# Project and output stages pipelined over the sequences, and the wide layer's q and k in two fp32r parts instead of three bf16 parts

## What is computed

```python
def wide(x, Wq, Wk, Wv, Wff, bff):            # 16 heads of 8 features, B, T, D = 4, 1024, 128 here
    q = x @ Wq.T * (1.0 / sqrt(D));  k = x @ Wk.T;  v = x @ Wv.T       # x is the layer norm of the residual
    scores = einsum('bqhd,bkhd->bhqk', q, k)                            # per head 1024 x 1024
    return einsum('bhqk,bkhd->bqhd', softmax(scores), v).reshape(B, T, D) @ Wff.T + bff

def nested(x, ...):                           # 8 heads of 16 features; x is the layer norm of the residual
    for e in range(4):                        # token block e of 256 uses only the first 128 >> e features
        xn = layernorm(x_e, norm_w, norm_b);  m = 128 >> e
        q_e = xn[..., :m] @ q_w[:, :m].T + q_b     # k and v alike
    attn = softmax(q k^T * D ** -0.5) v       # over all 1024 tokens, per head
    return x + attn_e[..., :m] @ o_w[:m, :m].T + o_b[:m]        # x here is the layer norm too
```

## Time and profile before

| what | value |
|---|---|
| median of 3 runs | 3489.55 us (3488.01 to 3509.23) |
| the profiled execution, its time | 3490.88 us |
| its span | 3489.2 us |
| mean granted TensorE clock | 0.886 of full |
| TensorE busy | 3009.2 us (86%) |
| VectorE busy | 2549.8 us (73%) |
| ScalarE busy | 2145.4 us (61%) |
| GpSimd busy | 274.4 us (8%) |

### The profile page before, as it was taken

The page is one execution under the profiler, slowest core; times in us unless marked ns, Lnnn a source line. Parts: engine busy times, 40 slices in busy tenths (PEclk is TensorE's granted clock), DMA queues, the critical chain, the costliest instruction groups (busy, mean ns, idle before and its releaser), DMA issues. The chain is left out here.

```text
span 3489.2 us, 54392 instructions
## 1 busy us (share of the span) xinstructions
PE 3009.2 (86%) x19914; PEld 1749.3 (50%) x19914; DVE 2549.8 (73%) x3990; ACT 2145.4 (61%) x3771; POOL 274.4 (8%) x373
## 2 busy tenths in 40 slices
PE   6757999848999999856999979979999777769998
PEld 4533444422333333332444457668888555558886
DVE  5657999389999999556999434447777777767776
ACT  2214888515988888712888711228888444458887
POOL 0060000050000000050000001020000000020000
PEclk9956999767999999955999968969999888879999
DMA  1042221021000010033221010021111000021111
GB/s 27 5 100 52 38 38 20 5 83 27 20 20 20 20 21 19 2 65 91 38 38 20 2 26 1 0 61 47 46 46 46 5 1 0 1 74 46 46 46 58
DMA packets 76544, 115.13 MB, mean 33 GB/s; under 512 B 13552, under 2 KB 38160, under 8 KB 76304
## 3 DMA queue, kind: packets, MB, share of 16 engines
q1 hardware_dynamic: 76304, 111.97, 13.6%
HBM read 85.72 MB, written 25.43 MB: 32 GB/s over the span
## 5 line engine op out<-in xcount | busy, mean ns | idle before, releaser
L729 DVE TENSOR_REDUCE nested_a_halves<-banks 128x2 f32<-128x1024 f32 x512 | 617.3, 1222 | 62.5 <-PE banks L825 59.4
L779 ACT ACTIVATE nested_a_p<-banks 128x512 f32<-128x512 f32 x1024 | 553.7, 597 | 116.1 <-PE banks L855 97.1
L729 DVE TENSOR_REDUCE wide_a_halves<-banks 128x2 f32<-128x1024 f32 x512 | 593.4, 1216 | 33.3 <-PE banks L825 33.3
L779 ACT ACTIVATE wide_a_p<-banks 128x512 f32<-128x512 f32 x1024 | 554.0, 598 | 45.2 <-PE banks L855 33.9
L1524 DVE TENSOR_TENSOR mix_e_h_low<-mix_e_h,mix_e_h_high 128x512 fp32r<-128x512 f32 x512 | 349.6, 688 | 174.9 <-ACT mix_e_h_high L1630 166.9
L1647 ACT ACTIVATE mix_e_h<-banks,mix_b_folded 128x512 f32<-128x512 f32 x512 | 353.7, 691 | 103.4 <-PE banks L1701 103.0
L868 PE MATMUL banks<-nested_a_p,nested_values 128*32 128x256 f32 x4096 | 326.5, 398 | 0.0
L868 PE MATMUL banks<-wide_a_p,wide_values 128*32 128x256 f32 x4096 | 321.4, 392 | 0.0
L1630 ACT ACTIVATE mix_e_h_high<-mix_e_h 128x512 fp32r<-128x512 f32 x512 | 319.3, 624 | 0.0
L825 PE MATMUL banks<-nested_k_stack,nested_q_stack 48*128 48x512 f32 x1024 | 270.6, 523 | 39.0 <-DVE nested_a_halves L729 20.9
L855 PE MATMUL banks<-nested_q_stack,nested_k_stack 50*128 50x512 f32 x1024 | 252.0, 422 | 10.9 <-ACT nested_a_p L779 9.9
(11 more groups left out here) (366 smaller groups left out, 4469.3 us busy)
## 6 DMA issues: line engine op xcount, KB each, us to landing
mix_e_gate<-mix_gates_t SPq DMA_DIRECT2D x128, 256.0 KB, 3.1
nested_q_stack<-nested_q_parts SPq DMA_DIRECT2D x96, 128.0 KB
nested_q_parts<-nested_p_q_cut SPq DMA_DIRECT2D x16, 512.0 KB
nested_k_parts<-nested_p_k_cut SPq DMA_DIRECT2D x16, 512.0 KB
nested_k_stack<-nested_k_parts SPq DMA_DIRECT2D x32, 256.0 KB
wide_q_stack<-wide_q_parts SPq DMA_DIRECT2D x192, 32.0 KB
nested_k_stack<-nested_k_parts SPq DMA_DIRECT2D x32, 128.0 KB
mix_raw_w<-L_ffn_w_t SPq DMA_DIRECT2D x8, 512.0 KB, 7.6
```

Of the source, the lines that this page charges most:

```text
L729: dve.tensor_reduce(halves[:, half, i, 2 * a:2 * a + 2], bank[:, at:at + 2, :], AX, ALU.max).then_inc(maxed, 1)
L779: act.activation(p[:, kt % 4, j, :], bank[:, ST + n % RING, :], ACT.Exp, scale=scale).then_inc(probs, 1)
```

## The change

In all three layers the project and output stages are written out over the sequences and keep two buffers of each tile. VectorE normalises two sequences ahead; GpSimd's fills are gone, and ScalarE writes the ones (`ones`, three instructions of 2048 columns, and `fill_pads`) instead; ScalarE cuts the high part of q and k directly out of PSUM (`cut_high`) and VectorE makes the rest from PSUM (`cut_rest`), so the whole copies are gone; in the nested layers `first` and GpSimd's addition of it become eight ScalarE instructions a sequence (`grow_rows`). TensorE turns sequences 0 and 1 before it projects 0. SyncE stores 0 and 1, then loads 0 and 1, then stores 2 and 3. The output stage turns straight out of `mixed`, with two sets of PSUM banks.

The wide layer is given fp32r: its q and k are two parts and three products, 3 x 8 = 24 rows (26 with the shift), still in tiles of 64 rows; a load is 10 DMAs instead of 18, and a sequence's stores four DMAs of 512 KB. Its score and shifted matmuls have as many columns, and as many of them are issued, as before.

```diff
@@ class Heads @@
-        self.span = min(n for n in (32, 64, 128) if n >= self.rows + 2)
+        self.span = min(n for n in (64, 128) if n >= self.rows + 2)
...
-        self.mixed = core.sbuf(ctx, "mixed", [P, self.total, TILES, self.gw])
+        self.mixed = core.sbuf(ctx, "mixed", [P, B, TILES, D])
...
-        self.parts_out = core.sem("parts_out")
+        self.parts_out = [core.sem(f"parts_out{k}") for k in range(2)]
@@ project_stage, SyncE @@
                 store(0)
-
-                sp.wait_ge(ones_set, 1)
-                sp.wait_ge(parts_out, 32 * hd.parts)
+                store(1)
+                sp.wait_ge(ones_set, hd.SLOTS)
+                sp.wait_ge(parts_out[0], 32 * hd.parts)
                 for n in range(2):
                     hd.load(sp, n)
-                with sp.Fori(1, B) as it:
-                    store(it)
+                for b in range(2, B):
+                    store(b)
@@ project_stage, GpSimd @@
-                values = hd.values[:].rearrange("p n i c -> p (n i) c")
-                pool.memset(values, 0.0).then_inc(v_set, 1)
...
-                pool.memset(ones, 1.0).then_inc(v_set, 1)
...
-                pool.memset(hd.plain(hd.k_stack[:]).rearrange("r k s t -> r (k s t)"), 1.0).then_inc(ones_set, 1)
...
+                for b in range(B):
+                    factors(b)
                 pool.wait_ge(w_in, 16 * NW)
...
+                for b in range(B):
+                    add_bias(b)
@@ project_stage, VectorE @@
-                def cut_parts(it, n, whole):
...
-                    dve.wait_ge(qk_copied, it * 4 + 2 * (n + 1))
-                    wait_past(dve, parts_out, it * 32 * hd.parts)
-                    dve.tensor_copy(parts[n][:, 0, :], whole[:]).then_inc(cut, 1)
-                    dve.wait_ge(cut, done + 1)
-                    if hd.parts == 2:
-                        dve.tensor_tensor(parts[n][:, 1, :], whole[:], hd.plain(parts[n][:, 0, :]),
-                                          ALU.subtract).then_inc(cut, 1)
-                        return
...
+                def cut_rest(b, n):
+
+                    for c in range(chunks):
+                        done = 4 * b + 2 * n + c
+                        dve.wait_ge(high_cut, done + 1)
+                        high = hd.plain(parts[n][:, b % 2, 0, cols(c)])
+                        whole = bank[:, 2 + 2 * n + c, :]
+                        if hd.parts == 2:
+                            wait_past(dve, parts_out[b % 2], b // 2 * 32 * hd.parts)
+                            dst = parts[n][:, b % 2, 1, cols(c)]
...
+                            dve.tensor_tensor(dst, whole, high, ALU.subtract).then_inc(rest_cut, 1)
...
+                moments_of(0)
+                moments_of(1)
+                normalise(0)
+                moments_of(2)
+                moments_of(3)
+                normalise(1)
+                dve.wait_ge(w_in, 16 * NW)
+                for b in range(B):
+                    cut_rest(b, 0)
+                    cut_rest(b, 1)
...
+                    if b + 2 < B:
+                        normalise(b + 2)
+                    store_values(b)
@@ project_stage, ScalarE @@
+                def grow_rows(b):
+
+                    act.wait_ge(factored, (b + 1) * FACTORS)
+                    act.wait_ge(normed, (b + 1) * TILES)
+                    for i in range(TILES):
+                        row = x[:, b * TILES + i, :]
+                        act.activation(row, row, ACT.Identity, bias=fall[:, b, i:i + 1],
+                                       scale=grow[:, b, i:i + 1]).then_inc(grown, 1)
+
+                def cut_high(b, n):
+
+                    wait_past(act, parts_out[b % 2], b // 2 * 32 * hd.parts)
+                    for c in range(chunks):
+                        act.wait_ge(projected, b * 6 + (2 * n + c + 1))
+                        dst, src = parts[n][:, b % 2, 0, cols(c)], bank[:, 2 + 2 * n + c, :]
...
+                            act.activation(dst, src, ACT.Copy).then_inc(high_cut, 1)
...
+                for k in range(hd.SLOTS):
+                    ones(hd.k_stack[:, k], [hd.slabs, T]).then_inc(ones_set, 1)
+                act.wait_ge(w_in, 16 * NW)
+                copy_turned(0)
+                copy_turned(1)
+                for b in range(B):
+                    if masked:
+                        grow_rows(b)
+                    for n in range(2):
+                        cut_high(b, n)
...
+                    if b + 2 < B:
+                        copy_turned(b + 2)
...
+                    fill_pads(b)
@@ project_stage, TensorE @@
+                pe.wait_ge(w_in, 16 * NW)
+                turn(0)
+                turn(1)
+                for b in range(B):
+                    project(b)
+                    if b + 2 < B:
+                        turn(b + 2)
@@ attend_stage, SyncE (and the same on ScalarE) @@
-                sp.wait_ge(hd.parts_out, 32 * hd.parts * B)
+                for k in range(2):
+                    sp.wait_ge(hd.parts_out[k], 16 * hd.parts * B)
@@ output_stage @@
-                        dve.tensor_copy(m_[:, :, g * hd.gw:(g + 1) * hd.gw], src).then_inc(staged, 1)
...
+                            src = bank[:, 4 + b % 2 * 2 + c, (lo - 4 * c) * P:(hi - 4 * c) * P].rearrange(
...
+                            last = pe.transpose(bank[:, b % 2 * 2 + c, i * P:(i + 1) * P], hd.mixed[:, b, 4 * c + i, :],
+                                                core.ident[:])
...
+                turn(0)
+                turn(1)
@@ plan @@
-            lambda: heads_layer(core, "wide", 16, wide, False, BF16),
+            lambda: heads_layer(core, "wide", 16, wide, False, F32R),
```

More of the change, by code:

```diff
@@ L519, in _ @@
-                pool.wait_ge(v_set, 2)
-                pool.memset(hd.plain(hd.k_stack[:]).rearrange("r k s t -> r (k s t)"), 1.0).then_inc(ones_set, 1)
-                pool.wait_ge(ones_set, 1)
-                with pool.Fori(1, B - 1) as it:
-                    residuals(it)
-                    factors(it + 1)
-                residuals(B - 1)
-                pool.wait_ge(residual, B * TILES * (2 if masked else 1))
+                        row = x[:, b * TILES + i, 0:m]
+                        pool.tensor_tensor(row, row, out_bias[:, 0:m], ALU.add).then_inc(biased, 1)
@@ new lines, in cut_rest @@
+                def cut_rest(b, n):
[7 more added lines that the diff above has]
+                            dst = parts[n][:, b % 2, 1, cols(c)]
+                        else:
+                            wait_past(dve, last_cut, 2 * b + n - 1)
+                            wait_past(dve, second_cut, 2 * b + n - 1)
+                            dst = rest[:, n, cols(c)]
+                        if masked:
+                            bias = (q_bias, k_bias)[n]
+                            dve.scalar_tensor_tensor(dst, whole, bias[:], high, ALU.add,
+                                                     ALU.subtract).then_inc(rest_cut, 1)
+                        else:
+                            dve.tensor_tensor(dst, whole, high, ALU.subtract).then_inc(rest_cut, 1)
@@ L565, in store_values, with cut_last @@
+                def cut_last(b, n):
+                    dve.wait_ge(second_cut, 2 * b + n + 1)
+                    wait_past(dve, parts_out[b % 2], b // 2 * 32 * hd.parts)
+                    dve.tensor_tensor(parts[n][:, b % 2, 2, :], rest[:, n, :], parts[n][:, b % 2, 1, :],
+                                      ALU.subtract).then_inc(last_cut, 1)
+                def store_values(b):
                     for c in range(2):
-                        dve.wait_ge(projected, it * 6 + (5 + c))
+                        dve.wait_ge(projected, b * 6 + (5 + c))
@@ new lines, in cut_second, with fill_pads @@
+                def cut_second(b, n):
+                    act.wait_ge(rest_cut, 4 * b + 2 * n + 2)
+                    act.activation(parts[n][:, b % 2, 1, :], rest[:, n, :], ACT.Copy).then_inc(second_cut, 1)
+                def fill_pads(b):
+                    pads = hd.values[:, b * hd.groups:(b + 1) * hd.groups].rearrange(
+                        "p g i (j r) -> p (g i j) r", r=32)[:, :, hd.width:32]
+                    ones(pads, [hd.groups * TILES * hd.GROUP, 32 - hd.width]).then_inc(pads_set, 1)
@@ L795, in _ @@
                 copy_shifts(0)
-                act.wait_ge(hd.parts_out, 32 * hd.parts * B)
+                for k in range(2):
+                    act.wait_ge(hd.parts_out[k], 16 * hd.parts * B)
                 for u in range(UNITS):
@@ L954, in _ @@
             def _(act):
-                with act.Fori(0, B) as it:
+                for b in range(B):
                     for c in range(2):
-                        act.wait_ge(turned, it * 2 + (c + 1))
-                        act.wait_ge(projected, it * 2)
-                        act.activation(m_t[:, c * BANK:(c + 1) * BANK], bank[:, c, :], ACT.Copy).then_inc(copied, 1)
+                        act.wait_ge(turned, b * 2 + (c + 1))
```

(23 more changed lines are left out.)

241 lines of the change are left out of this document (110 added, 131 removed).

## The result

The changed kernel takes 3865 us (median of 4 runs, 3852.63 to 3865.74) where the kernel before takes 3495.6 (4 runs). The ratio is 1.104, with a 95% interval of 1.100 to 1.109: slower by a tenth. Its profiled execution took 3852.63 us, the fastest of the four, with a span of 3850.9 us, 361.7 more than before.

A forecast was written before the change was run, and what follows sets the result against it. TensorE was taken to bound the attention loops nearly throughout, waits the project stages. To the profiled 3490.9 us came +486 for the wide loop at the low clock and -98 for the pipelining: 3879 us, range 3600 to 3950.

The forecast's parts named there:

- The clock: Wide attention loop: starts at 0.50 and, with 24 and 26 rows, doesn't rise; low clock throughout given 0.75.
- the mixture keeps whichever level it finds: Nested1's and the wide layer's last units: 50-row pairs and value matmuls stay at the clock they find, 0.50 or 1.00.
- the fall in nested1's last unit: Nested1's attention loop: the clock, full before, fell to 0.50 after one pause of TensorE.
- The price at the low clock: Wide attention loop: 2.16 us a step, 36.1 us a unit, 1142 us against 656, so +486 us.
- fp32r at full clock: Wide attention loop: fp32r costs 1.53 us a unit over 32 units, +49 us, if nothing else moves.
- rival 1: Wide loop: the clock rises as now, fp32r costs +49 us, the rest saves 98, total 3442 us; chance 0.13.
- The project stages of the nested layers: Nested1 and nested2: first exponential 28 us earlier in each, bounds 10 and 36, waiting for all stores to land.
- The wide project stage: Wide layer: first exponential at 787 us instead of 814.6, 27 us gained, bounds 12 and 34.
- The output stages: All three layers: no staging copy and overlapping sequences gain 5 us each, bounds 2 and 9, from TensorE's idle time.
- The chances: Whole kernel: faster by over 1% 0.17, within 1% 0.02, slower 0.81.
- the full-clock cases: Wide loop at full clock: with the cost of fp32r (3442 us, chance 0.13) or without it (3393 us, 0.04).

The follow-up runs named there:

- pads_48: The changed kernel with 24 rows of zeros (ones in one k row) after the wide layer's 24, giving 48 and 50 rows: 3412.2 us, ratio 0.975.
- pads_first4: The changed kernel with wide rows moved up 32 partitions over zeros, units 0 to 3 contracting 56 and 58 rows, the rest 24 and 26: 3799.7 us, ratio 1.088.
- wide_bf16: The changed kernel with the wide layer back in three bf16 parts (48 and 50 rows), everything else as changed: 3374.6 us, ratio 0.965.
- pads_36: The changed kernel with 12 rows of zeros added in the wide layer, giving 36 and 38 rows: 3714.0 us, ratio 1.063.
- twice_48: The changed kernel with the wide layer's three products loaded twice (48 rows of data) and the exponentials' scale halved: 3447.7 us, ratio 0.985.

## Why the prediction was right

The forecast of 3879 us lies 14 us above the median and 26 above the profiled execution on which the sum was made.

- **The clock.** The step that carried the forecast, that the loop with 24 and 26 rows doesn't rise from the level at which it starts, held: 0.50 over 1148.7 us. What follows the rows was shown by pads_48, where rows of zeros alone bring the clock back. The reason that I gave beside it, that the mixture keeps whichever level it finds, was wrong: pads_first4 handed a high clock to a step with 24 and 58 rows, and it was lost after 18 us without a pause. So the loop most likely stays low because it can't hold the other level, and not only because it starts there. What makes the clock fall stays open. I had put the fall in nested1's last unit on one pause of TensorE; in wide_bf16 and pads_48 nested1's last unit, the same instructions, has the same pause (busy 3.23 of 4.00 us from 612 to 616) and stays at 1.00. And in the kernel before the clock came back there from 656 us on (0.96), with the mixture unchanged. That I drew the right conclusion for the new loop from this stretch was partly luck.
- **The price at the low clock.** 2.16 us a step, 36.1 us a unit: measured 2.16 and 36.16. The loop was put at 1142 us and took 1148.7, +492 instead of +486.
- **fp32r at full clock**, the term of rival 1, was 1.53 us a unit and +49; pads_48 measured 1.54, and +51 for the loop, which also stood longer at the low clock. Rival 1's 3442 us was the time with the clock up; pads_48, which is that case, took 3412 (its profiled execution 3423). The stages gained about 40 us beyond my figure, and that execution gave back 20 of them in nested2's loop (373.1 us against 352.9), where the clock rose 35 us after the first exponential.
- **The project stages of the nested layers**: -28 each, measured -30.5 and -30.2. The size was right and the path was not. I had the first exponential wait for the last store to land, then for load(2)'s issues and the shift rows behind them. The last store had landed by 258.2, earlier than the 263 to 270 given, and load(2)'s issues were over at 262.7, yet SyncE then waited until 266.7 for the shift rows. The chain was the issue of the last store (over at 242.8), 0.8 us to the first score pair, and 29.8 us of row maxima, shift rows and first shifted pairs, as long as before. What got shorter by 30.5 us is the stretch up to the first score pair, 82.8 us instead of 113.3. That the path through the landing, worked out in advance, gave nearly the same time is luck.
- **The wide project stage**: -27, measured -39.8, beyond my bound of -34. This is the term that was most mis-sized. I had the drain end near 775 and the first exponential at 787 us on the old time axis; it came 81.3 us after the stage's start, which is 774.8 on that axis. The rate was taken from nested1 (145 to 158 GB/s); here stores and loads moved at 219 GB/s between 664.0 and 709.6 us, and all had landed 63 us into the stage, at 756.7 on the old axis. And as in the nested layers it was the issue of the last store, over at 697.2, that let the first score pair start at 697.9. Against wide_bf16 some 12 us of the gain come with two parts instead of three, which I had counted only as bytes and not as work for ScalarE and VectorE.
- **The output stages**: -5 each, measured -15.6, -8.9 and -13.8. I bounded the gain by TensorE's idle time of 7.8 and 9.1 us and forgot that in the nested layers its busy time at a clock of 0.60 would shrink as well: after the change the stretches stand at 0.95, 0.88 and 0.91, and TensorE's busy time in nested1's fell from 21.4 to 12.3 us. The wide one stood at 0.93 before, and its gain is mostly idle time (9.1 to 1.6 us).
- **Not foreseen**: nested2's loop took 7.7 us longer, with its clock rising about 31 us after the first exponential instead of 9. Its instructions are the same in all variants, and it took from 352.9 us (the kernel before) to 373 (pads_48, pads_36); differences of up to 20 us between two executions here can be this alone.
- **The chances**: the cases that I put down as slower add up to 0.83 and not 0.81, and the 0.02 for no change would have to come out of the 0.17 of the full-clock cases.

The sum was close because its largest term was right. The stages gained 139 us and not 98, which put into the sum gives 3838; the wide loop (+6.4), nested2's loop (+7.7) and the rest (+0.4 together) bring it to the 3852.6 of the profiled execution. The other three executions took some 12 us more than that one.

**The rule of the Trainium skill** ("TensorE: Matmul & The Clock Gate", Part 1: The HAM clock gate), by which the gate follows how busy TensorE has been, does not describe this loop: TensorE was busy 1146.5 of 1148.7 us, at 0.50.

The version that beats both kernels is wide_bf16, the pipelined stages with the wide layer left in three bf16 parts: 3374.6 us, 3.5% under the kernel before. Most of what the pipelining gave is in it; the fp32r part costs 492 us in one loop and saves 12 in one stage, by the difference between the two wide project stages.

## What to carry to other kernels

Halving the rows of a matmul that is already short of them didn't make it quicker here, and it can take the clock away from everything that runs on TensorE beside it; rows of zeros cost about 1 us of the project stage here and brought it back (pads_48 against the change: 441 us in one loop). Before a change of operand shape, look in the profile for a stretch where TensorE is fully busy at a granted clock of 0.50, and price the new loop with the step measured there. Look at what the first instruction of the next stage waits for: here it was the issue of the last store, and not its landing. And in a short stage at the low clock, idle time isn't the bound of what overlap can gain: the busy time may shrink too.

## What the runs showed of the hardware that I had not expected

- With 36 and 38 rows the same stream alternated between the two levels for 987 us: stretches at 1.00 lasted 48 us (four of them) or 3 us (three), those at 0.50 31 or 140 us after the first, and the last 63 us stood at 1.00. With 24 and 26 rows it never rose, with 48 and 50 it rose after 18 us and stayed.
- Zeros counted as data did: after their rise pads_48 ran at 1.00 and twice_48 at 0.97, its clock falling for some us at a time.
- The same instructions in nested1's last unit, with the same pause of 0.8 us ahead, fell to 0.50 for 14 us in the kernel before and stayed at 1.00 in wide_bf16 and pads_48.
- The first score pair of an attention stage started 0.7 or 0.8 us after SyncE had issued the last store of the project stage, in every layer before and after, though the stores landed 3 to 15 us later.
- At the low clock the stream of 24-row pairs and that of 48-row pairs have the same step, 2.16 us, and a tile 32 or 64 partitions from its neighbour makes no difference (3846 and 3865 us, ratios 1.100 and 1.104).
- In the mixed units of pads_first4, where a 24-row pair sits at partition 32 of its tile and a 58-row pair at 0, the step was 1.43 us at full clock (781.09 to 782.52) and 2.46 at half (802.56 to 805.02), where steps with equal pairs took 1.24 and 2.16. It wasn't tried which of the two, the position or the difference in rows, makes them overlap less.
